# Weight squares half a step sooner in two feed-forward steps, norms ahead of exponentials in two late units, one addition to X behind a low half

## What is computed

```python
x = x + L0_xattn(layernorm(x), ctx)      # 32 query heads, 8 key/value heads, rotated queries and keys, softmax
x = x + L0_ffn(layernorm(x))             # weights unpacked from 4 bits; silu(gate) * up, then down; inner width 1376
x = x + L1_xattn(layernorm(x), ctx)      # 32 and 8 heads, normalised queries and keys, softmax
x = x + L1_ffn(layernorm(x))             # routed to the 8 best of 128 slots, gated
```

## Time and profile before

| what | value |
|---|---|
| time, median of 3 runs | 2380.14 us (2379.61 to 2381.68) |
| the profiled execution: time | 2379.67 us |
| the profiled execution: span from first to last instruction | 2377.8 us |
| mean granted TensorE clock | 0.997 |
| PE busy | 2342.0 us, 98% |
| DVE busy | 1743.2 us, 73% |
| ACT busy | 1287.3 us, 54% |
| POOL busy | 1289.7 us, 54% |

### The profile page before, as it was taken

One profiled execution on the slowest core, in us unless ns is written; L12 is line 12 of the kernel. 1 busy time (PEld: TensorE's weight loads), 2 busy tenths in 40 slices (PEclk: granted clock), 3 DMA queues, 4 the chain that ended last, 5 costly groups with the idle time before them and its releaser, 6 DMA issues.

```text
span 2377.8 us, 46196 instructions
## 1 busy us (share of the span) xinstructions
PE 2342.0 (98%) x18012; PEld 1326.5 (56%) x18020; DVE 1743.2 (73%) x3256; ACT 1287.3 (54%) x2507; POOL 1289.7 (54%) x1046
## 2 busy tenths in 40 slices
PE   8899999999999999999999999999999999999998
PEld 4555555555555555444666655555555555555555
DVE  8887887888888898756887676667666666666666
ACT  7766665656555555424454564555555555554544
POOL 4656556666666666237853454445555555446542
PEclk9999999999999999999999999999999999999999
DMA  6121121312121111110102011222121212221101
GB/s 215 45 45 36 45 54 28 125 28 54 30 58 30 43 40 25 32 45 27 36 29 99 30 32 28 45 54 63 37 63 37 63 37 63 54 44 28 23 19 71
DMA packets 217912, 116.60 MB, mean 49 GB/s; under 512 B 169408, under 2 KB 192608, under 8 KB 216672
## 3 DMA queue, kind: packets, MB, share of 16 engines
q1 hardware_dynamic: 217696, 113.64, 19.0%
HBM read 65.81 MB, written 8.39 MB: 31 GB/s over the span
## 4 chain that ended last, share of the span: by engine, by line
PE 79%; DVE 5%; ACT 1%; issue 1%; POOL 1%; DVEq 0%; ACTq 0%; POOLq 0%
PE PB L960 24%; PE PB L912 22%; PE PB L896 6%; PE PB L1072 5%; PE PB L1129 4%; PE PB L937 3%; PE PB L1002 3%; PE PB L880 2%; PE PB L1083 2%; PE PB L868 2%; PE PB L981 1%; PE PB L1031 1%; DVE SML L2141 1%; DVE X L2354 0%; PE PB L1182 0%
## 5 line engine op out<-in xcount | busy, mean ns | idle before, releaser
L912 PE MATMUL PB<-XTB,WB 128*128 128x512 f16 x3072 | 680.6, 380 | 2.5 <-DVE WB L2135 1.5
L960 PE MATMUL PB<-WB,AR 128*128 128x512 f16 x3072 | 681.4, 379 | 1.0 <-DVE AR L2339 1.0
L960 PEld LDWEIGHTS PB<-WB,AR 128*128 128x128 f16 x3072 | 297.5, 98 | 353.4 <-issue 3.1
L912 PEld LDWEIGHTS PB<-XTB,WB 128*128 128x128 f16 x3072 | 297.6, 98 | 347.5 <-issue 8.0
L2354 DVE SCALAR_TENSOR_TENSOR X<-PB,SML,X 128x512 f32<-128x512 f32 x256 | 190.0, 747 | 179.1 <-PE PB L960 172.8
L2974 POOL TENSOR_TENSOR AR<-AR,SML 128x512 f32<-128x512 f32 x128 | 144.6, 1151 | 314.3 <-DVE SML L2324 314.3
L1636 ACT ACTIVATE AR<-PB 128x512 f16<-128x512 f32 x256 | 131.7, 600 | 234.8 <-PE PB L1002 234.2
L2228 DVE TENSOR_TENSOR AR<-PB,AR 128x512 f16<-128x512 f32 x128 | 88.1, 690 | 164.5 <-ACT AR L1599 164.5
L2963 POOL TENSOR_TENSOR AR<-AR,CST 128x512 f32<-128x512 f32 x128 | 180.7, 1412 | 29.6 <-ACT AR L1546 29.5
L2954 POOL TENSOR_TENSOR AR<-AR,CST 128x512 f32<-128x512 f32 x32 | 47.8, 1494 | 247.2 <-ACT AR L1525 247.2
L2968 POOL TENSOR_TENSOR AR<-AR 128x512 f32<-128x512 f32 x128 | 174.1, 1360 | 12.7 <-DVE AR L2190 2.9
(11 more groups left out here) (315 smaller groups left out, 4110.3 us busy)
## 6 DMA issues: line engine op xcount, KB each, us to landing
STG<-in_wo SPq DMA_DIRECT2D x14, 1024.0 KB
STG<-in_wq SPq DMA_DIRECT2D x13, 1024.0 KB
STG<-in_qw_gu SPq DMA_DIRECT2D x40, 128.0 KB
STG<-in_ctxT SPq DMA_DIRECT2D x4, 1024.0 KB
X<-in_x SPq DMA_DIRECT2D x4, 1024.0 KB, 10.8
kept<-CTB SPq DMA_DIRECT2D x4, 1024.0 KB, 7.5
CTB<-kept SPq DMA_DIRECT2D x4, 1024.0 KB, 6.5
out_x<-X SPq DMA_DIRECT2D x16, 256.0 KB, 2.3
```

The costliest lines, as they stand in the source:

```text
L912: m = pe.do.matmul(b[:, :], wq[x][:, k, h * 128:(h + 1) * 128], XT[y][c][:, k, :], start=n == 0, stop=n == 11)
L960: m = pe.do.matmul(b[:, :], AT[x][:, h, t * 128:(t + 1) * 128], wo[y][:, h, :], start=n == 0, stop=n == 11)
```

## The change

The place of one ACT stage (the squares) moves from slot 3 to slot 2 of step (s, 2), for s = 2 and 3, and the place of "peak", on PE and DVE, moves from slot 1 of step (s, 3) to slot 3 of step (s, 2). In layer 1, ACT does the first half norm of units 2 and 4 ahead of the exponentials in place of behind them and the second half of the values. In the turn-over, DVE's addition of output tile 3 of unit 29 to X moves from the end of unit 30 to a place behind the four low halves of unit 30's weighed values. No operation is added or taken out.

```diff
@@ plan_ln
-            for half, (norm, turn, low) in enumerate((("k" if L == 0 and u < 5 else 0, 2, 2), (3, 5, last))):
+            for half, (norm, turn, low) in enumerate((("k" if u < 5 else 0, 2, 2), (3, 5, last))):
@@ places of the feed-forward stages
         for s in (2, 3):
-            plan_prep_f(w(1, 0, s - 1), (s, 2, 3), (s, 3, 1), (s, 3, 2), (s + 1, 0, 3), (s + 1, 1, 1))
+            plan_prep_f(w(1, 0, s - 1), (s, 2, 2), (s, 2, 3), (s, 3, 2), (s + 1, 0, 3), (s + 1, 1, 1))
@@ scalar, front
                     else:
+                        side(1, beside, "k")
                         exponent(1, beside)
                         values_1(u, 1)
                         side(1, beside, 0)
@@ vector, units
                     for t in range(4):
-                        if u > 0:
+                        if u > 0 and (L, u, t) != (0, NU - 2, 3):
                             output(L, u - 1, t)
@@ vector, turn_over
                 u = NU - 1
                 weighed(0, u - 1)
+                output(0, u - 2, 3)
                 soft_max_0(u)
```

## The result

| | before | changed |
|---|---|---|
| time, median of ten runs each on one chip | 2380.53 us (2379.19 to 2382.26) | 2386.72 us (2385.82 to 2390.29) |
| ratio, 95% interval | 1 | 1.0027 (1.0019 to 1.0035) |
| the profiled execution: time | 2379.67 us | 2386.68 us |
| its span, mean granted clock | 2377.8 us, 0.997 | 2384.9 us, 0.994 |

The change costs 6.2 us. These are the waits of PE in the changed kernel, over the whole span: line, what it waited for, us in total, times, longest us.

What follows compares the result with a forecast made beforehand. PE, busy 98%, was taken as the bound. Stalls of +2.3 and +2.4, addition +1.2 and norms 0 gave +5.9 us (2386.0); 2.1 us of clock made it +8.0, 2388.1 us; range 2384.3 to 2392.3.

Steps and rivals of the forecast that it cites:

- the rival in which the clock holds: Both stalls come but the clock stays at full: +5.9 us, 2386.0 (2385.2 to 2386.6); chance 0.25.
- First stall: Step (2, 3): PE's unpacking waits in bank 4 for DVE's late reduction of the peak, 3.88 us; net +2.3 us.
- The covers: The weight's load lands before the squares, which end before ACT's gate at 1221.92; cost 0 to 0.3 us.
- the third rival: ACT's squares of 1.90 us delay the gates and the stall grows: 2391 us and more; chance 0.03 above 2391.5.
- Second stall: Step (3, 3): PE's unpacking again waits for DVE's reduction of the peak, 3.98 us; net +2.4 us.
- the signs: Expected in the changed profile: L1055 waits for DVE's reduction twice, over 3 us each, near 1163 and 1226.
- the rival in which the delay is taken back: DVE, not PE, bounds steps (2, 3) and (3, 3): near 2382 us; chance 0.17 together with DVE in time.
- The credit of 1.6 us for each step: Steps (2, 3) and (3, 3): the old peak matmul and its waits go, 1.6 us less in each.
- a quarter of a microsecond: What may come back where PE waits a little for DVE at the end of step (2, 3).
- The addition: Turn-over: output tile 0 of unit 30 waits in bank 2 for the moved addition, +1.2 us; -0.7 if not bound.
- The norms: Layer 1, units 2 and 4: PE's norm wait goes, but DVE's low half is late; 0 each, -0.45 as other end.
- The clock: The granted clock falls behind the two new idle times, 0 to 2.5 us each; 2.1 us taken for both.

Runs made afterwards that it cites:

- e4_peak_bank3: The changed kernel with the peaks of the two weights in bank 3 in place of bank 4; 2381.28 us, 1.0001 against the kernel before.
- e6_step3_only: The kernel before with only the squares and peak of step (3, 2) moved; 2384.49 us, 1.0017.
- e5_step2_only: The kernel before with only the squares and peak of step (2, 2) moved; 2383.45 us, 1.0013.
- e7b_squares_bank0: The kernel before with only the squares moved, peaks left in their slot but in bank 0 in place of bank 4; 2378.18 us, 0.9989.
- e8_all_mended: Kernel before with squares earlier, addition moved, output tiles 0 and 1 of unit 30 in swapped banks, norms and DVE's second half of values earlier; 2377.41 us, 0.9988.
- e13_all_filled: The changed kernel with unused matmuls filling PE's idle time at both stalls and in the turn-over; 2384.73 us, 1.0014 against the kernel before.
- e11_stall_filled: The changed kernel with 14 and 8 unused matmuls filling PE's two stalls; 2386.28 us, 1.0022 against the kernel before.
- e1: The kernel before with the moved addition alone; 2380.78 us, 0.9998.
- e12: The changed kernel run again with no edit; 2387.53 us, 1.0026 against the kernel before.
- e2: The kernel before with the squares and peaks of both steps moved, nothing else; 2384.72 us, 1.0015.

## Why the prediction was right

The forecast was 2388.1 us, the time 2386.72. Against the kernel before beside it the loss was 6.2 us, where 8.0 had been forecast. The time alone wouldn't decide between the forecast (2386.5 to 2391.5) and the rival in which the clock holds (2385.2 to 2386.6), since it lies where they meet; the low clock behind the first stall does.

**First stall: right in mechanism and size.** Bank 4, peak_ok, the two additions ahead of the reduction: 3.83 us against 3.88, and e4_peak_bank3 shows the cause. The covers held: the squares don't delay the gates, so the third rival didn't come.

**Second stall: right in mechanism, mis-sized.** The term was 3.98 us, and 2.46 was measured, a wait of 2.33 us where the signs had named over 3. The term took DVE's lateness from the kernel before for both places. DVE is late because it lags behind PE, and the first stall gives it time, as does the low clock behind it; e6_step3_only has the 3.7 us back. This is the rival in which the delay is taken back, for a part of the second term.

**The credit of 1.6 us for each step: right in size, but not a credit of the edit in both.** In (3, 3) 1.52 us came back. But e5_step2_only, whose peak there didn't move, has 1.47 us back too: the first stall, there with a low clock behind it, takes these waits away by itself. In (2, 3) it was 0.79 + 1.25 = 2.0 us, of which 0.41 lies where the wait for L2466 was, which I had put at "a quarter of a microsecond". There e4_peak_bank3 and e7b_squares_bank0 show that without a stall this credit is nearly worthless, because DVE bounds the end of the step. In the changed kernel it counted only since DVE had caught up.

**The addition: right.** +1.06 and +1.08 us against +1.2, by bank 2, as the swap of banks in e8_all_mended shows. That it could cost the clock too, I had not considered: I looked for a fall only at the two long stalls.

**The norms: near 0, as said.** The low half is late next, as the rows of the weight loads had shown; 0.17 us for each unit came through of the 0.45 that I had put as the other end.

**The clock: near in size, with luck.** 2.1 us were forecast. In the changed kernel's profile it took 2.43 us behind the first stall, and about 0.6 of it came back at the second. The term priced a fall by one that had cost 2.5 us; behind the stalls here it was 1.67 us in four cases and 2.43 and 2.74 in one each. "Nearer to one fall than to none" describes the median; single executions have more or less. All four profiles with an unfilled first stall show a fall behind it; of the four with an unfilled second stall two do, so that both would usually pay, as I had reckoned, held for the first alone. What the Trainium skill says in "TensorE: Matmul & The Clock Gate", "Part 1: The HAM clock gate (the 'warmup' mystery)", that the monitor doesn't run in step with the kernel, agrees with these runs: the same code lost the clock at the first stall in one execution and at both in another.

So the sum without the clock was 5.9 and is 4.2 in e13_all_filled. It was too high by 0.9 us in the second stall, 0.4 in the credit of step (2, 3), 0.3 in the norms and 0.1 in the addition. In the profiled execution of the changed kernel, where a low clock shortens the second stall further, it came out as 3.45. That this execution reached 7.0 us above before in spite of it is luck: 1.19 us of it are the clock in the first 20 us, which no one could have worked out of the change.

## What to carry to other kernels

When an operation moves in one queue, list the buffers that it holds and who asks for them next in every other queue: here both losses were a bank whose next user had become the very next instruction, and another bank number took the larger one away. A lag of one engine behind another is a stock that a stall works off, so a second stall of the same kind is shorter behind a first, and small waits further on go by themselves; and a wait taken away pays only up to where the lagging engine becomes the bound. Try the half of an edit that only uses idle time by itself: the squares alone made the kernel 0.12% faster (0.02% to 0.21%), and the peaks turned that into a loss.

## What the runs showed of the hardware

The granted clock fell after a single idle time of 2.11 us in e11_stall_filled (0.66 from 960 to 965), behind 48 matmuls of 64 columns and with full work from there on. It stayed at 1.00 after the same idle time in four other profiles (the changed kernel, e1, e4 and e12). Near 1385 it fell behind an idle time of 1.3 us and 32 matmuls of one column in seven of fourteen profiles, at a place that is the same in all. A fall cost 1.7 us at the turn-over, 1.67 us (e2, e12), 2.43 us (changed) or 2.74 us (e5) at the first stall, 1.67 us at the second (e6, e12) and 1.5 to 1.6 us near 1385. The second stall, of 2.33 us, cost nothing in one execution of the changed kernel and showed 0.73 in another. Where the clock was low behind the first stall, the second was up to 0.6 us shorter. The mean granted clock of each run went with its time: in e12_changed_again 2384.8 to 2386.3 us at 0.996 and 2387.3 to 2389.1 at 0.994, from the same code.
